# Cross-attention and quantized FFN on one core: the order of each engine's slots written anew

## The chip, the cores and the metric

One core of one Trainium2 chip. The time is the device time of one execution in microseconds (us); every table and row below is in us unless it says ns.

## The reference, cut to what matters

The input `x` is 64 x 64 rows of 256 (4096 rows, 32 tiles of 128 rows; a tile holds two sequences). All matrices are fp32.

```python
q_r    = layernorm(x) @ A            # Wq, w_kc_q, W_qr (and W_kr) are folded into one matrix per head, 16 heads
scores = q_r @ rope(kv).T            # per sequence and head, 64 x 64
attn   = softmax(scores)             # minus the row maximum, exp, divided by the row sum
ctx    = attn @ rope(kv)             # 64 columns per head
x      = x + ctx @ Bfold             # w_kc_kv and Wo folded: 1024 -> 256
h      = bitlinear(layernorm(x), w1) # rmsnorm, rows quantized to 8 bits, w1 to {-1,0,1}: 256 -> 1024
y      = x + bitlinear(gelu(h), w2)  # the same with w2: 1024 -> 256
```

## The kernel before, in words

All loops are unrolled in Python. Each engine has its own instruction stream, written out by hand as a loop over **slots** `n`, with semaphores between the streams. An engine works through its stream strictly in the order written: an instruction that waits holds back everything behind it on that engine. Slot `n` starts with the scores of tile `n`; older tiles are at later steps in the same slot. In a slot the stages are, with the tile that each works on before the change:

- **TensorE (PE)**: `scores(n)` (L707); two `queries` groups of 12 matmuls (L690 to L692) for coming tiles; `turned(n)` (L721), one transpose that turns the partial row maxima of tile n and the partial row sums of tile n-1 at once; `project(n-3)` (L754 to L756), 24 matmuls in two halves; `shifts(n)` (L734), which subtracts the row maxima from the scores in PSUM; `contexts(n-1)` (L744), which needs the division of tile n-2 to be through, since both use the two banks CB; `up(n-7)` (L776), 4 matmuls; `down(n-10)` (L786), 8 matmuls. Both ups of a pair lie around the border between an odd and an even slot.
- **VectorE (DVE)**: `quadrant_max(n)` (L923, two instructions), then `x_max(n-4)`, in even slots `norms` (14 small dependent instructions, L996, L196 to L201, L999, L1001), then `row_max(n)` (L936, tile nmax), `row_sum(n-1)` (L942, L946, tile ri), `divide(n-2)` (L953, two instructions, tile cr), `residual(n-3)`, maxima and scales of the FFN, `quadrant_sum(n)` (L930), `finish(n-10)` (L1007).
- **SyncE (SP)** issues the DMAs in order: `shift_rows(n)` (L343, nmax to shift), `rinv_rows(n-1)` (L351, the reciprocal sums to DRAM), `rinv_spread(n-1)` (L360, back from DRAM to 128 partitions, tile rb, waits for L351 to have landed), the transposes `turn_x` (L365) and `turn_g` (L370), the stores (L374). In slots 1 to 6 a 512 KB load of x (`load_x`) is issued between L343 and L351, and in slots 3 to 5 two `swap_kv` too.
- **ScalarE (ACT)**: `exp(n)`, `ctx_hi(n-2)` (L550), the copies of queries, `gelu(n-7)` (L565), squares. Exp and Gelu each need a table load when they follow the other.
- **GpSimd (POOL)**: `ctx_lo(n-2)` (L440), `centre(n-3)`, `x_round`, `g_round` (L463, L466), `norm_x` (L315), the rotation of kv (`rope`, L240 to L244) and rounding of w2 in the first slots.

Tile n's division thus needs `row_sum(n)` in slot n+1, the two DMA steps L351 and L360 in slot n+1, and stands in slot n+2:

```python
def divide(u, b):
    if b == 0:
        dve.wait_ge(sem["contexts"], u + 1)
        dve.wait_ge(sem["rinv_spread"], 32 * (u + 1))
```

Down uses columns 256 to 511 of the bank O, whose other half holds the projection. Four rounded FFN rows (g) and two of each transposed tile are kept. The loop runs over NT + 10 = 42 slots.

## Time and profile before

| what | us |
|---|---|
| median of 3 runs (455.26 to 457.75) | 455.36 |
| the profiled execution, device time | 457.08 |
| its span, first to last instruction | 454.9 |
| PE busy | 393.1 (86%) |
| DVE, ACT, POOL busy | 330.5, 257.8, 255.2 |
| mean granted PE clock | 0.957 |

Busy time is what the profiler records per instruction; matmuls overlap. A releaser behind "<-" is the instruction or DMA that ended an engine's idle time. R(n) stands below for the start of `row_max(n)`, the one L936 instruction of slot n; 32 of them mark the slots from R(0) = 39.2 to R(31). The span then has three parts: up to R(9) the start, with loads and few FFN steps; R(9) to R(31) the steady part; and the tail.

### The profile page before, as it was taken

To read this page: it belongs to the slowest core of one execution; us is meant where nothing else is said; L and a number is where in the kernel's file an instruction comes from. 1 tells how busy PE (TensorE), PEld (TensorE's weight loads), DVE (VectorE), ACT (ScalarE), POOL (GpSimd) and SP (SyncE) were. 2 spreads that over 40 slices of the span, in tenths; PEclk is the share of its full clock that TensorE was granted. 3 is DMA by queue.
4 is the path that set the end of the run, shared out by engine and by line. 5 is a ranking of instruction groups with operands and counts; after the bars stand their busy time and mean duration, and the time that the engine had idled before them with its cause. 6 is when DMAs were issued, how large, how long until landed. Compare 5 with 4: busy or idle time off the path is not lost.

```text
span 454.9 us, 8971 instructions
## 1 busy us (share of the span) xinstructions
PE 393.1 (86%) x2855; PEld 282.0 (62%) x2870; DVE 330.5 (73%) x873; ACT 257.8 (57%) x477; POOL 255.2 (56%) x321
## 2 busy tenths in 40 slices
PE   9799889794988999989999999999999997876554
PEld 7587557572665776767676767676767674464222
DVE  0364867584798789887878787878787888877564
ACT  1155543332667676675758585858585857556340
POOL 1209447994365656667373738373837373767543
PEclk9899999996999999999999999999999999999665
DMA  8993254443213232424262434252424253443333
GB/s 216 404 333 128 56 142 117 119 117 92 64 52 78 62 79 71 102 48 106 73 107 71 108 73 105 72 107 71 108 72 107 72 107 77 102 127 81 78 97 92
DMA packets 65533, 48.81 MB, mean 107 GB/s; under 512 B 50384, under 2 KB 55888, under 8 KB 65104
## 3 DMA queue, kind: packets, MB, share of 16 engines
q1 hardware_dynamic: 64880, 44.72, 37.8%
q10 hardware_dynamic: 608, 3.54, 2.3%
q8 instruction: 23, 0.38, 0.4%
q14 instruction: 22, 0.18, 0.2%
HBM read 31.98 MB, written 4.46 MB: 80 GB/s over the span
## 4 chain that ended last, share of the span: by engine, by line
POOL 34%; issue 31%; PE 15%; DMA 7%; DVE 6%; SPq 4%; ACT 1%; POOLq 1%; ACTq 0%; DVEq 0%
POOL cl L440 7%; POOL tq L463 6%; POOL qb L466 6%; POOL xa L455 3%; DMA wq_s<-wq 3%; POOL xq L458 3%; POOL yc L450 2%; POOL xn L315 2%; PE hps L786 2%; POOL w_s L478 2%; SPq L365 2%; DMA shift<-nmax 2%; PE ps L744 2%; PE ps L690 2%; DVE cr L953 1%
## 5 line engine op out<-in xcount | busy, mean ns | idle before, releaser
L440 POOL TENSOR_TENSOR cl<-cr,ch 128x512 fp32r<-128x512 f32 x64 | 80.3, 1277 | 131.0 <-ACT ch L550 131.0
L690 PE MATMUL ps<-xh,ah 128*128 128x256 f32 x256 | 75.6, 295 | 4.9 <-ACT g L565 4.5
L754 PE MATMUL hps<-bh,ch 128*128 128x256 f32 x256 | 76.7, 300 | 1.4 <-POOL cl L440 1.4
L534 ACT ACTIVATE qf<-ps 128x512 f32<-128x512 f32 x64 | 37.5, 586 | 65.4 <-PE ps L692 65.4
L755 PE MATMUL hps<-bl,ch 128*128 128x256 f32 x256 | 72.2, 282 | 0.0
L756 PE MATMUL hps<-bh,cl 128*128 128x256 f32 x256 | 72.2, 282 | 0.0
L691 PE MATMUL ps<-xl,ah 128*128 128x256 f32 x256 | 71.9, 281 | 0.0
L692 PE MATMUL ps<-xh,al 128*128 128x256 f32 x256 | 71.8, 280 | 0.0
L550 ACT ACTIVATE ch<-cr 128x512 fp32r<-128x512 f32 x64 | 39.3, 631 | 55.0 <-DVE cr L953 55.0
L690 PEld LDWEIGHTS ps<-xh,ah 128*128 128x128 f32 x256 | 48.2, 188 | 26.7 <-issue 25.8
L786 PE MATMUL hps<-w2q,qt 128*128 128x256 bf16 x256 | 39.1, 303 | 17.3 <-DMA qt<-qb 12.8
L786 PEld LDWEIGHTS hps<-w2q,qt 128*128 128x128 bf16 x256 | 25.0, 107 | 44.7 <-issue 24.4
L930 DVE TRANSPOSE_TENSOR_REDUCE red<-pe 128x16 f32<-128x512 f32 x64 | 41.6, 689 | 14.9 <-ACT pe L545 14.7
L565 ACT ACTIVATE g<-ps,scl 128x512 f32<-128x512 f32 x64 | 41.0, 683 | 19.6 <-PE ps L776 19.4
L923 DVE TRANSPOSE_TENSOR_REDUCE red<-hps 128x16 f32<-128x512 f32 x64 | 41.4, 685 | 12.6 <-PE hps L707 12.3
L754 PEld LDWEIGHTS hps<-bh,ch 128*128 128x128 f32 x256 | 48.4, 189 | 3.2 <-POOL cl L440 1.8
L755 PEld LDWEIGHTS hps<-bl,ch 128*128 128x128 f32 x256 | 48.4, 189 | 0.1
L756 PEld LDWEIGHTS hps<-bh,cl 128*128 128x128 f32 x256 | 48.3, 189 | 0.0
L692 PEld LDWEIGHTS ps<-xh,al 128*128 128x128 f32 x256 | 48.3, 188 | 0.0
L691 PEld LDWEIGHTS ps<-xl,ah 128*128 128x128 f32 x256 | 48.2, 188 | 0.0
L953 DVE TENSOR_TENSOR cr<-ps,rb 128x512 f32<-128x512 f32 x64 | 41.2, 686 | 7.2 <-DMA rb<-rinv_d 4.0
L776 PE MATMUL ps<-w1q,xqt 128*128 128x512 bf16 x113 | 35.1, 403 | 9.5 <-DVE xs L958 5.1
(136 smaller groups left out, 830.2 us busy)
## 6 DMA issues: line engine op xcount, KB each, us to landing
rb<-rinv_d SPq DMA_DIRECT2D x64, 256.0 KB, 3.9
xs<-x SPq DMA_DIRECT2D x8, 512.0 KB, 4.3
out<-yo SPq DMA_DIRECT2D x32, 128.0 KB, 3.5
wq_s<-wq SPq DMA_DIRECT2D x2, 1024.0 KB, 14.4
w_s<-w_t SPq DMA_DIRECT2D x2, 1024.0 KB, 7.2
wo_s<-wo_t ACTq DMA_DIRECT2D x1, 2048.0 KB, 11.1
wk_a<-wk_t SPq DMA_DIRECT2D x2, 512.0 KB, 7.3
kvs<-kvn SPq DMA_DIRECT2D x8, 128.0 KB, 4.1
```

Of the source, the lines that this page charges most:

```text
L440: pool.tensor_tensor(cl[:, u % 2, :, b * S:(b + 1) * S], cr[:, :, b * S:(b + 1) * S], ch[:, u % 2, :, b * S:(b + 1) * S].bitcast(F32), ALU ...
L565: act.activation(g[:, t % GB, 512 * half:512 * half + 512], turn_bank("h", t, half), ACT.Gelu, scale=hscale(scl, t)).then_inc(sem["gelu_do ...
L690: pe.matmul(o, ah[:, c, cols], xh[:, k % 2, c, :], start=(c == 0), stop=False)
L691: pe.matmul(o, ah[:, c, cols], xl[:, k % 2, c, :], start=False, stop=False)
L692: m = pe.matmul(o, al[:, c, cols], xh[:, k % 2, c, :], start=False, stop=(c == KC - 1))
L754: pe.matmul(O[:, 0:D], c_h, bh[:, hp, :], start=(hp == 0), stop=False)
L755: pe.matmul(O[:, 0:D], c_h, bl[:, hp, :], start=False, stop=False)
L756: m = pe.matmul(O[:, 0:D], c_l, bh[:, hp, :], start=False, stop=(hp == HP - 1))
L786: m = pe.matmul(O[:, D:2 * D], qt[:, t % 2, c, :], w2q[:, c, :], start=(c == 0), stop=(c == FC - 1))
L923: dve.tensor_reduce(red[:, u % 2, 16 * b:16 * b + 16], SB[b].rearrange("p (k s) -> p k s", s=32), AX.X, ALU.max, apply_transpose=True).the ...
L930: dve.tensor_reduce(red[:, (u + 1) % 2, 64 + 16 * b:80 + 16 * b], pe32[:, u % 2, b, :].rearrange("p (k s) -> p k s", s=32), AX.X, ALU.add, ...
L953: dve.tensor_tensor(cr[:, :, b * S:(b + 1) * S], CB[b].rearrange("p (h s) -> p h s", s=S), rb[:, b, :].rearrange("p (h s) -> p h s", s=S), ...
```

## The change

Every stream's slot is written in another order, and the distance of a tile behind its scores shrinks (NT + 6 = 38 slots):

- DVE: `divide(n-2)` is first in the slot, ahead of `quadrant_max(n)`; in odd slots the two `finish` of tiles n-6 and n-7 stand ahead of it. `residual(n-2)` is last (it was n-3, in the middle). In even slots `x_max(n-3)` and `x_scale` stand between `quadrant_max(n)` and `row_max(n)`.
- PE: `contexts(n-1)` moves from the end of the slot to after the scores and one queries group (even) or the two ups of tile n-5 (odd), ahead of `turned(n)`. Ups of tiles n-5 and n-4 both in odd slots, downs of n-5 and n-6 both in even slots; `project(n-2)`, one half or both behind the shifts. Downs of odd tiles go to the bank T. `x_t`, `fold_out` and `b_hi`, `b_lo` move by a slot.
- ACT: the four gelus of a pair in the odd slot with `ctx_hi` between; a dummy Gelu at the end of even slots loads the table.
- POOL: the rms norms move here from DVE, with `pow` in place of the Newton steps (six instructions); `x_round(n-4)`, `x_round(n-3)` in even slots, both `g_round` in odd ones. `norm_x(4)`, `norm_x(5)` run ahead of the loop.
- SP: `turn_g(n-5)` ahead of `shift_rows` in even slots, at the end in odd ones; `turn_x` behind `rinv_spread`; two stores ahead of `shift_rows` in odd slots. The issues `shift_rows(n)`, `load_x`, `swap_kv`, `rinv_rows(n-1)`, `rinv_spread(n-1)` keep their order.

```diff
@@ sync
-                for n in range(LAST + 1):
-                    if n % 2 == 0 and tile(n - 6):
-                        turn_x(n - 6)
-                        turn_x(n - 5)
-                    if n % 2 and tile(n - 10):
-                        turn_g(n - 10)
+                for n in range(LAST):
+                    if n % 2 == 0 and tile(n - 5):
+                        turn_g(n - 5)
+                    if n % 2 and tile(n - 7):
+                        store(n - 6)
+                        store(n - 7)
                     if tile(n):
                         shift_rows(n)
...
                     if tile(n - 1):
                         rinv_rows(n - 1)
                         rinv_spread(n - 1)
-                    if tile(n - 11):
-                        store(n - 11)
+                    if n % 2 == 0 and tile(n - 4):
+                        turn_x(n - 4)
+                        turn_x(n - 3)
+                    if n % 2 and tile(n - 5):
+                        turn_g(n - 5)
@@ tensor
                     if tile(n):
                         scores(n)
...
+                    if n % 2 and tile(n - 5):
+                        up(n - 5, 0)
+                        up(n - 5, 1)
+                    if n % 2 == 0 and k < NB:
                         queries(k, b)
+                    if tile(n - 1):
...
+                        contexts(n - 1)
+                    if n % 2 and tile(n - 5):
+                        up(n - 4, 0)
                     if n <= NT:
                         turned(n)
...
+                    if n % 2 == 0 and tile(n - 6):
+                        down(n - 5)
+                        down(n - 6)
@@ vector
                 for n in range(LAST):
...
+                    if n % 2 and tile(n - 7):
+                        finish(n - 6)
+                        finish(n - 7)
+                    if tile(n - 2):
+                        divide(n - 2, 0)
+                        divide(n - 2, 1)
                     if tile(n):
                         quadrant_max(n, 0)
                         quadrant_max(n, 1)
-                    if tile(n - 4):
-                        x_max(n - 4)
-                    if n % 2 == 0 and 0 <= (n - 6) // 2 < NB + 2:
-                        norms((n - 6) // 2)
+                    if n % 2 == 0 and tile(n - 4):
+                        x_max(n - 3)
+                        x_scale((n - 4) // 2)
                     if tile(n):
                         row_max(n)
                     if tile(n - 1):
                         row_sum(n - 1)
-                    if tile(n - 2):
-                        divide(n - 2, 0)
-                        divide(n - 2, 1)
...
+                    if tile(n - 2):
+                        residual(n - 2)
```

## Rows read from the trace of the kernel before

**Rows 1.** A stretch of two slots: busy time by engine, granted clock (--windows).

```profile
core 0: us, PE busy (x) PEld busy (x) DVE busy (x) ACT busy (x) POOL busy (x), PEclk, DMA share, GB/s
240.00:263.00 23.00, 21.86 (x173) 16.21 (x166) 18.12 (x47) 15.87 (x30) 13.09 (x16) 1.00 0.37 88
```

**Rows 2.** Timeline of VectorE, slots 18 to 20: start, length, what [idle before <-releaser].

```profile
245.12 0.28 DVE L936 TENSOR_REDUCE nmax<-hps 32x64 fp32r<-32x128 f32 x1 [0.32 <-PE hps L721]
...
255.79 0.28 DVE L936 TENSOR_REDUCE nmax<-hps 32x64 fp32r<-32x128 f32 x1 [1.42 <-PE hps L721]
...
257.00 1.29 DVE L953 TENSOR_TENSOR cr<-ps,rb 128x512 f32<-128x512 f32 x2
...
268.18 0.28 DVE L936 TENSOR_REDUCE nmax<-hps 32x64 fp32r<-32x128 f32 x1 [0.32 <-PE hps L721]
```

**Rows 3.** Timeline of SyncE's issues in slot 18.

```profile
246.92 0.81 SPq L351 DMA_DIRECT2D rinv_d<-ri  x2
248.75 1.31 SPq L360 DMA_DIRECT2D rb<-rinv_d  x2
```

**Rows 4.** DMA issues of the whole run: KB each, median us from issue to landing.

```profile
rb<-rinv_d SPq DMA_DIRECT2D x64, 256.0 KB, 3.9
...
xqt<-xq SPq DMA_TRANSPOSE x32, 2.9
qt<-qb SPq DMA_TRANSPOSE x32, 2.8
```

**Rows 5.** Timeline of VectorE in the start: slots 1, 2, 3, 4 and 9.

```profile
49.37 0.28 DVE L936 TENSOR_REDUCE nmax<-hps 32x64 fp32r<-32x128 f32 x1 [0.42 <-PE hps L721]
...
56.84 0.28 DVE L936 TENSOR_REDUCE nmax<-hps 32x64 fp32r<-32x128 f32 x1 [0.42 <-PE hps L721]
...
60.35 1.29 DVE L953 TENSOR_TENSOR cr<-ps,rb 128x512 f32<-128x512 f32 x2 [2.33 <-DMA rb<-rinv_d]
...
68.63 0.28 DVE L936 TENSOR_REDUCE nmax<-hps 32x64 fp32r<-32x128 f32 x1 [1.09 <-PE hps L721]
...
80.56 1.29 DVE L953 TENSOR_TENSOR cr<-ps,rb 128x512 f32<-128x512 f32 x2 [1.67 <-DMA rb<-rinv_d]
...
139.16 0.28 DVE L936 TENSOR_REDUCE nmax<-hps 32x64 fp32r<-32x128 f32 x1 [1.31 <-PE hps L721]
```

**Rows 6.** Timeline of SyncE's issues in slot 2, after its nmax.

```profile
62.53 1.31 SPq L360 DMA_DIRECT2D rb<-rinv_d  x2
```

**Rows 7.** Timeline of TensorE: contexts after a division, shifts of slot 6, an up.

```profile
61.79 0.61 PE L744 MATMUL ps<-pe,kvn 64*64 64x512 f32 x1 [0.42 <-DVE cr L953]
...
108.27 1.22 PE L734 MATMUL hps<-shift,em 128*128 128x512 f32 x2 [6.37 <-DMA shift<-nmax]
...
261.93 0.59 PE L776 MATMUL ps<-w1q,xqt 128*128 128x512 bf16 x2
```

**Rows 8.** Chain that ended last, in order of time: start, length, what.

```profile
110.34 1.91 PE ps L744 x8
...
133.40 1.02 PE ps L744 x8
...
450.37 1.88 PE hps L786 x8
```

**Rows 9.** Two us of slot 6, columns as in rows 1.

```profile
109.00:111.00 2.00, 2.00 (x10) 1.04 (x12) 1.27 (x3) 1.68 (x3) 0.11 (x1) 0.50 0.52 203
```

**Rows 10.** Timeline of GpSimd in slot 0: a rotation starts; later the norms.

```profile
40.27 1.28 POOL L240 TENSOR_TENSOR kvn<-kv_s,turn 128x512 f32<-128x512 f32 x1
...
44.25 2.07 POOL L315 TENSOR_SCALAR xn<-xs,rstd,nmean 128x256 f32<-128x256 f32 x2
```

**Rows 11.** Timeline of VectorE: the last nmax, of slot 31.

```profile
391.35 0.28 DVE L936 TENSOR_REDUCE nmax<-hps 32x64 fp32r<-32x128 f32 x1
```

**Rows 12.** Groups by line and form: xcount, busy, mean ns of one, idle before.

```profile
L440 POOL TENSOR_TENSOR cl<-cr,ch 128x512 fp32r<-128x512 f32 x64 | 80.3, 1277 | 131.0 <-ACT ch L550 131.0
...
L975 DVE TENSOR_REDUCE amax<-g 128x1 f32<-128x1024 f32 x32 | 37.4, 1212 | 0.0
...
L463 POOL TENSOR_SCALAR tq<-g,c 128x1024 f32<-128x1024 f32 x32 | 35.8, 1119 | 13.3 <-DVE c L982 10.9 <-POOL qb L466 2.4
```

More of the change, by code:

```diff
@@ L53, with norm_count @@
 YR = 4
-LAST = NT + 10
-NORM_STEPS = RSQRT_OPS + 3
+LAST = NT + 6
+def norm_count(j):
+    return sum(6 if 1 <= i < NB else 4 for i in range(j + 1))
 def build(nc, x, kv, wq, wk_t, wqr, wkr_t, wkv, wo_t, w1_t, w2_t, consts, out):
@@ L259, in build @@
             k, b = n // 2 + 1, 2 * (n % 2)
-            if n % 2 == 0 and tile(n - 7):
-                USES += [("h", n - 7, 0), ("h", n - 7, 1)]
+            if n % 2:
+                USES += [("h", t, half) for t in (n - 5, n - 4) if tile(t) for half in range(2)]
             if k < NB:
                 USES.append(("q", k, b))
-            if n % 2 and k + 1 < NB:
-                USES.append(("x", k + 1))
+            if n % 2 == 0 and n // 2 + 2 < NB:
+                USES.append(("x", n // 2 + 2))
             if k < NB:
@@ L269, in build @@
                 USES.append(("k", (n + 2) // 4))
-            if n % 2 and tile(n - 7):
-                USES += [("h", n - 7, 0), ("h", n - 7, 1)]
         def hscale(a, t):
@@ L424, in _ @@
                         swap_kv(n - 2)
-                    if n % 2 and tile(n - 9):
-                        turn_g(n - 9)
                     if tile(n - 1):
@@ L502, in _ @@
                 rope(pool, 1, sem["rope_steps"]).then_inc(sem["rope_done"], 1)
+                norm_x(pool, 4)
+                norm_x(pool, 5)
                 for n in range(LAST):
@@ L657, in _ @@
                         exp(n, 1)
+                    if n % 2 and k < NB:
+                        q_out(k, b + 1)
+                    if n % 2 and tile(n - 5):
+                        square_g(n - 5)
                     if turns(n):
@@ L904, in _ @@
                         fold_out(1)
-                    if turns(n):
-                        kv_t((n + 2) // 4)
-                    if tile(n - 1):
-                        if n == 1:
-                            pe.wait_ge(sem["b_lo_done"], 2)
-                        contexts(n - 1)
-                    if tile(n - 10):
-                        down(n - 10)
-                    if n % 2 and tile(n - 7):
-                        up(n - 7, 1)
+                    if n == 1:
+                        fold_out(3)
             @block.vector
@@ L1102, in _ @@
                         ternary(n)
+                    if n == 1:
+                        b_lo(2)
+                    if n % 2 == 0 and n // 2 + 2 < NB:
+                        x_lo(dve, n // 2 + 2)
+                    if n % 2 and tile(n - 3):
+                        x_max(n - 3)
+                    if n % 2 and tile(n - 5):
+                        for t in (n - 5, n - 4):
+                            g_max(t)
+                            g_scale(t)
+                    if n % 2 == 0 and 2 <= n < 14:
+                        statistics(dve, 4 + 2 * n, 8 + 2 * n)
                     if tile(n):
@@ L1105, in _ @@
                         quadrant_sum(n, 1)
-                    if tile(n - 10) and (n % 2 or not tile(n - 8)):
-                        finish(n - 10)
                     if n == 0:
                         b_lo(0)
-                    if n < 3:
-                        b_lo(n + 1)
-                    if 2 <= n < 14:
-                        statistics(dve, 4 + 2 * n, 6 + 2 * n)
+                        b_lo(1)
+                    if n == 1:
+                        b_lo(3)
+                    if tile(n - 2):
+                        residual(n - 2)
 def _constants():
```

244 lines of the change are left out of this document (119 added, 125 removed).

## The prediction

> **What bounds the kernel now.** I read the busy table first, then the windows, then the timeline of each engine in the same two slots, and last the DMA issues. In the steady part two slots take 268.18 - 245.12 = 23.06 us, and TensorE is busy for 21.86 of 23.00 us at full clock, DVE for 18.12, POOL for 13.09 [rows 1, 2]. So TensorE bounds it, with about 1.1 us of idle in two slots. That is all that any new order can win there: 11 pairs of slots lie between R(9) and R(31), so at most 11 x 1.2 = 13 us.
>
> The softmax chain runs beside it, and what matters is how much slack it has. From row_max(n) the chain to the division of tile n-1 is: reciprocal sums issued to DRAM 1.80 us after R(n) (246.92 - 245.12), the spread issued 1.83 later (the issue has waited for the first landing), its second DMA half a pair of issues later (0.65), and 3.9 to 4.2 until it has landed [rows 2 to 4]. I take 4.0, so the division of n-1 can start at R(n) + 8.3. Before the change the division comes later than that: in slot 18 the rows of tile 17 have landed at R(18) + 8.3 = 253.4, and its division starts in slot 19 at 257.00, behind R(19) = 255.79 [rows 2]. The slack is 3.6 us, and it exists because the division stands behind quadrant_max and row_max of its slot.
>
> In the start there is no such slack. DVE itself waits for rb in slot 2 (60.35, idle 2.33) and in slot 4 (80.56, idle 1.67). There R(1) = 49.37 leads to 60.35, a delay of 10.98, and R(3) = 68.63 to 80.56, a delay of 11.93 [rows 5]. For slot 2 the spread is issued at 62.53, 5.69 after R(2) = 56.84, which with 0.65 + 4.0 gives 10.4 [rows 5, 6]. The 2 to 3.6 us above 8.3 are the loads of x and the swaps of kv issued between L343 and L351.
>
> **The part that decides: the division first.** After the change row_max(n+1) stands behind divide(n-1), in order on DVE, and row_max(n) has to run before that division's data are on their way. So a loop closes: R(n) -> spread landed -> divide(n-1) -> quadrant_max(n+1) -> turned -> R(n+1). What each turn costs behind the landing:
> - Into an odd slot without ups: two divisions and two quadrant_max, 1.2 each pair to the next start and 1.3 to the last end, then transpose and start of nmax 0.35: 2.85. The two divisions' 1.29 stand in [rows 5]; quadrant_max I take equally long, since both read 128 x 512.
> - Into an odd slot with ups (n of 5 and more) TensorE is later than DVE: contexts wait for the division and start 0.15 after its end (61.79 against 60.35 + 1.29) [rows 5, 7], take 1.02 [rows 8], one up half takes 0.53 (261.93 to the scores of 262.46; the row's 0.59 is its length) [rows 7], then transpose and nmax 0.31: 3.3.
> - Into an even slot x_max and x_scale (0.7 together, an estimate from the small instructions) stand ahead of row_max: 3.15.
>
> **Steady part.** A pair of slots needs 2 x 8.3 + 3.3 + 3.15 = 23.05 us by the loop, against 23.06 now and 21.9 by TensorE. The gain that the denser TensorE order could bring is eaten by the loop. Over 22 slots 22 x 11.53 = 253.6 against 391.35 - 139.16 = 252.2 now [rows 5, 11]: **+1.4**.
>
> **Start.** norm_x(4) and (5) run ahead of the loop, 4 us earlier than before, but x_t(2) moves to slot 0, where TensorE gets to it about 39.2. The norms can start only at 40.3 and take 1.1 to 2.1 us [rows 10]; TensorE stands about 2.4 us, and with b_lo(1) ahead of contexts(0) and quadrant_max(1) the slot 1 slips: R(1) = 52.8 in place of 49.37, **+3.4**. Then the loop: delays to the division from R(1) to R(8) are 10.98, 10.4, 11.93, then 12.0 in slots 4 and 5 (loads and swaps as in slot 3), 10.4 in slot 6 (load only), 8.3 and 8.3: sum 84.3. The rest into R(2) to R(9) is 2 x 2.85 + 3 x 3.3 + 3 x 3.15 = 25.1. So R(9) = 52.8 + 109.4 = 162.2, against 139.16 now [rows 5]: **+23** with the 3.4.
>
> TensorE now idles 4 to 6 us in each of slots 2 to 6, waiting for the division before contexts. In slot 6 of the trace the granted clock is 0.50, the 1.2 GHz level, behind an idle of 6.37, and eight context matmuls take 1.91 in place of 1.02 [rows 7 to 9]. These lie in the loop, so I add 0.8 x 5 = **+4**. The Trainium skill (TensorE: Matmul & The Clock Gate, HAM oscillation) says the same of loops that wait for a DMA in each turn: the engine falls back to half clock every time. By that rule the whole 4 us are due, by the row of slot 6 alone only when the idle is as long as there; without it the start is +23.
>
> **Tail.** From R(31) = 0: division(30) at 8.3, contexts(31) end cold at 11.8, row_sum(31) 13.1, rb(31) lands at 13.1 + 1.85 + 0.65 + 4.0 = 19.6. Gelus of pair 28, 29 and ctx_hi stand between, ctx_lo (1.28) ends at 25.0. POOL then rounds g of 28 and 29 (4 x 1.1), 29.5; centre(31), x_max, x_scale, x_round to 33.0; transposed by 36.3 (two issues, 2.9). Up and gelu of 31 end at 38.9, its maximum and scale at 40.5, rounded 43.3, transposed 46.4 (2.8), two cold downs of 1.9, finish 0.5, store 2.1: 53.0 [rows 4, 8, 12]. Now it is 454.9 - 391.35 = 63.55 [rows 11]: **-10.5**. The shorter pipeline wins here: three to four tiles' FFN steps fewer are left.
>
> **Moves without a price.** The norms leave DVE: 14 small instructions in an even slot, which now end before nmax (it waits 0.32 for the transpose behind them [rows 2]), so nothing is won while that wait stays. On POOL six instructions, 2.3 us as an estimate with one pow of 1.0, lie in 10 idle us of a pair [rows 1]; if the cover goes, gelu of the next odd slot is late by at most that. The gelus in the middle of the odd slot push exp to R + 5.4, ahead of the next scores at R + 6.4; without that cover about 0.5 a pair. Downs in pairs, bank T, stores first in odd slots, turn_g ahead of shift_rows: rounded g is ready some 3 us before that issue; bounds 0 to +0.5 us a pair, I take 0. The number of table loads stays.
>
> **Sum.** 23 + 4 + 1.4 - 10.5 = +17.9, so the span goes from 454.9 to 472.8 and the profiled execution from 457.08 to 475.0. That execution lies 1.7 above the median of the three runs, so against 455.36 I predict **473 us**.
>
> **Rivals.**
> - A, the loop in the start only: rb lands quicker and the steady part falls to TensorE's 21.9. Then 473 - 12.7 - (cold clock) 4 = 456, or 460 if the cold stays. For it: rb takes 3.9 in the median with other traffic about. Against: the 4.2 of many spreads.
> - B, faster: no loop, the divisions find their rows landed as they do now in the steady part. Place: R to division in slots 1 to 8. Point of decision: a turn must average 11.4 us instead of 14.2, so the landing must be some 2.8 us earlier there. Then the start keeps its present 89.8 us less the stall of slot 6 (6.4 [rows 7], where the shifts wait behind other work of SyncE and DVE), and the tail's 10.5 come in whole: 455.4 + 3.4 + 1.4 - 10.5 - 6.4 = 443. Against: two waits for rb already stand in that stretch [rows 5].
> - C, worse: SyncE's order adds to the loop. If turn_g ahead of shift_rows, or transposes in front of it, cost 0.6 a slot over 22 slots, it is 473 + 13 = 486.
>
> **Chances.** Forecast 0.65, A 0.11, B 0.14, C 0.10. The range of 456 to 484 takes in the unknown bounds (cold clock 0 or 4, landing 3.9 or 4.2 over 30 turns = 9 us, steady part down to TensorE's bound) and leaves out B. About 1% is what a measurement tells from no change: slower by over 1% 0.79, within it 0.07 (the lower end of A and the upper of B), faster 0.14.
>
> **What would show it.** In the trace after: DVE cr waits for DMA rb in nearly every slot, some 1 to 5 us in slots 2 to 7; nmax follows nmax by 13 to 15 us in slots 1 to 6 and by 11.5 after slot 8; PE's contexts (L744 before) wait for cr; R(1) near 53, R(9) near 163 to 167, last nmax to the end near 53. Wrong if R(9) stays below 150, or if DVE doesn't wait for rb, or if pairs fall below 22.5 us.

## The result, and the profile after

| | before | after |
|---|---|---|
| median of 4 runs (lowest to highest) | 455.95 (455.26 to 457.75) | 504.77 (501.81 to 508.05) |
| the profiled execution, device time | 457.08 | 508.05 |
| its span | 454.9 | 506.2 |
| mean granted PE clock | 0.957 | 0.919 |

The ratio is 1.107, 95% interval 1.098 to 1.115: slower by 49 us. The direction is the predicted one. The size is not: 473 was forecast, with 484 as the upper end. The profiled execution, from which all rows below come, is the longest of its four and lies 3.3 above their median. One execution further below, of the kernel with single columns (499.96 us), was in the slow state and is left out of that kernel's median.

The start of row_max of slots 1, 9 and 31 splits both spans into the three parts that the prediction used. Timeline of VectorE after the change (start, length, what, idle before and its releaser), first the slots 1 and 2, then slots 9, 15 to 17 and 31. Here and in the fences below, rows in between are left out:

```profile
54.88 0.28 DVE L971 TENSOR_REDUCE nmax<-hps 32x64 fp32r<-32x128 f32 x1 [0.42 <-PE hps L745]
65.85 1.29 DVE L988 TENSOR_TENSOR cr<-ps,rb 128x512 f32<-128x512 f32 x2 [4.91 <-DMA rb<-rinv_d]
69.71 0.28 DVE L971 TENSOR_REDUCE nmax<-hps 32x64 fp32r<-32x128 f32 x1 [1.35 <-PE hps L745]
...
173.67 0.28 DVE L971 TENSOR_REDUCE nmax<-hps 32x64 fp32r<-32x128 f32 x1 [0.70 <-PE hps L745]
...
258.14 1.29 DVE L988 TENSOR_TENSOR cr<-ps,rb 128x512 f32<-128x512 f32 x2 [1.09 <-issue]
259.35 1.30 DVE L958 TRANSPOSE_TENSOR_REDUCE red<-hps 128x16 f32<-128x512 f32 x2
260.57 0.38 DVE L998 TENSOR_REDUCE amax<-yc 128x1 f32<-128x256 f32 x1
260.98 1.14 DVE L1004 SCALAR_TENSOR_TENSOR gm<-amax,level 128x2 f32<-128x2 f32 x1
262.24 0.28 DVE L971 TENSOR_REDUCE nmax<-hps 32x64 fp32r<-32x128 f32 x1
270.79 1.29 DVE L988 TENSOR_TENSOR cr<-ps,rb 128x512 f32<-128x512 f32 x2 [1.21 <-DMA rb<-rinv_d]
274.00 0.28 DVE L971 TENSOR_REDUCE nmax<-hps 32x64 fp32r<-32x128 f32 x1 [0.70 <-PE hps L745]
...
451.40 0.28 DVE L971 TENSOR_REDUCE nmax<-hps 32x64 fp32r<-32x128 f32 x1 [0.70 <-PE hps L745]
```

| part | before | predicted | after |
|---|---|---|---|
| R(1) | 49.37 | 52.8 | 54.88 |
| R(9) | 139.16 | 162.2 (+4 for the clock) | 173.67 |
| R(9) to R(31) | 252.2 | 253.6 | 277.7 |
| R(31) to the end | 63.55 | 53.0 | 54.8 |

So 34.5 us of the difference in the spans (51.3) arose in the start and 25.5 in the steady part, and the tail gave 8.7 back. Against [rows 2]: there the division comes 1.21 after the row_max of its own slot, with no idle before it; here it stands first in the slot and DVE idles before it. The list of waits of the whole run says it for all slots (us in total, times, longest):

```profile
DVE cr L988 <- issue: 35.3, 17, 6.6
...
PE ps L768 <- DVE cr L988: 30.7, 26, 4.9
...
PE ps L800 <- DMA xqt<-xq: 23.6, 13, 6.9
```

On the page the same wait has a second releaser, and "issue" only says that the profile shows none: the tile's own view gives `DMA rb<-rinv_d` 22.6 us in 13 times beside the 35.3 in 17, 30 waits in 32 divisions. In the start the chain that ended last shows the loop itself, here from slot 1 to 7, and with two rows from slot 11 (start, length, what):

```profile
57.41 2.97 DMA rinv_d<-ri
61.13 4.22 DMA rb<-rinv_d
67.28 1.98 PE ps L768 x8
72.36 3.15 DMA rinv_d<-ri
76.22 1.56 DMA rb<-rinv_d
77.80 2.80 issue
82.03 1.98 PE ps L768 x8
108.97 4.11 DMA xqt<-xq
113.52 1.49 PE ps L800 x3
115.01 1.92 PE ps L768 x8
...
146.98 1.79 PE ps L768 x8
...
191.18 4.97 DMA xqt<-xq
198.03 1.86 PE ps L768 x8
```

Store the reciprocals, spread them, contexts behind the division, and again: one turn a slot. In slots 5, 7 and 11 the last link is not the spread but the transposed x (`xqt`), which is issued behind the spread and which the ups ahead of contexts wait for. From slot 13 on the chain view runs along GpSimd, with gaps of up to 6.5 us that it calls "issue", and shows the loop no longer; for the steady part the waits above, the sum below and the experiments have to carry it. TensorE goes cold in the loop. Two windows of 2 us with contexts of slots 2 and 5, and one with the contexts of a warm slot (columns as in [rows 9]):

```profile
67.20:69.20 2.00, 1.92 (x9) 0.34 (x9) 1.16 (x2) 1.08 (x3) 1.91 (x2) 0.50 0.01 4
114.90:116.90 2.00, 2.00 (x10) 0.35 (x10) 0.46 (x1) 1.21 (x2) 0.57 (x1) 0.50 0.00 0
284.90:286.10 1.20, 1.05 (x8) 0.24 (x8) 1.20 (x3) 1.20 (x4) 1.05 (x1) 1.00 0.41 75
```

The clock is 0.50, the 1.2 GHz level, in both cold windows, and eight context matmuls take 1.98 and 1.92 in the chain where the warm ones take 1.05.

Two slots of the steady part, to be held against [rows 1], take 25.46 in place of 23.06 us, with the same work on TensorE. TensorE no longer bounds them:

```profile
262.24:287.70 25.46, 21.62 (x163) 15.86 (x163) 17.80 (x37) 15.26 (x30) 15.42 (x22) 1.00 0.39 80
```

**One turn, measured.** For each slot I read R to the division, and the division to the next R. Means over R(9) to R(31), 22 slots:

| | predicted | measured | slots | us |
|---|---|---|---|---|
| R to division | 8.3 | 8.95 (even), 8.85 (odd) | 22 | +13.2 |
| division to R of an odd slot | 3.3 | 3.47 | 11 | +1.9 |
| division to R of an even slot | 3.15 | 3.99 | 11 | +9.2 |

The sum is +24.3, and the miss in the steady part is 277.7 - 253.6 = 24.1. These terms cover the whole slot, so the sum has to come out; what it shows is where the miss sits. The +1.9 comes from the turns into two slots, 11 and 25, which took 4.66 and 4.60 where most take 3.21: there the ups waited 2.2 and 2.3 us for the transposed x, and the contexts behind them ran at a granted clock of 0.55 and 0.50. The experiments had to show that these terms are causes and not places where something else is waited out.

### The profile page after: what moved, and what is told of

The parts are those of the page before. It is cut to its first block, busy times and chain, and to the rows that moved or that the text cites. A ratio compares the mean times of both kernels' runs of the same rounds, so it can differ in the third digit from the quotient of the medians.

```text
span 506.2 us, 8902 instructions
## 1 busy us (share of the span) xinstructions
PE 407.0 (80%) x2854; PEld 294.7 (58%) x2870; DVE 302.9 (60%) x653; ACT 261.6 (52%) x499; POOL 292.2 (58%) x417
## 3 DMA queue, kind: packets, MB, share of 16 engines
q1 hardware_dynamic: 64880, 44.72, 36.7%
## 4 chain that ended last, share of the span: by engine, by line
issue 30%; POOL 30%; DMA 15%; PE 8%; SPq 8%; DVE 6%; POOLq 1%; ACT 1%; DVEq 0%
POOL cl L427 8%; POOL tq L450 6%; DMA rinv_d<-ri 5%; DMA rb<-rinv_d 4%; POOL qb L453 3%; SPq L329 3%; DMA wq_s<-wq 3%; DMA xqt<-xq 3%; PE ps L768 2%; POOL fw L474 2%; POOL xa L442 2%; POOL yc L437 2%; DVE cr L988 2%; SPq L346 2%; POOL xn L301 2%
## 5 line engine op out<-in xcount | busy, mean ns | idle before, releaser
L713 PE MATMUL ps<-xh,ah 128*128 128x256 f32 x256 | 78.0, 305 | 3.4 <-ACT g L579 3.1
L988 DVE TENSOR_TENSOR cr<-ps,rb 128x512 f32<-128x512 f32 x64 | 41.2, 686 | 57.9 <-issue 35.3
L780 PE MATMUL hps<-bh,cl 128*128 128x256 f32 x256 | 74.8, 292 | 0.0
L779 PE MATMUL hps<-bl,ch 128*128 128x256 f32 x256 | 74.8, 292 | 0.0
L768 PE MATMUL ps<-pe,kvn 64*64 64x512 f32 x128 | 41.6, 723 | 31.3 <-DVE cr L988 30.7
L713 PEld LDWEIGHTS ps<-xh,ah 128*128 128x128 f32 x256 | 50.5, 197 | 22.6 <-issue 12.6
L778 PEld LDWEIGHTS hps<-bh,ch 128*128 128x128 f32 x256 | 51.7, 202 | 8.9 <-POOL cl L427 7.6
L800 PE MATMUL ps<-w1q,xqt 128*128 128x512 bf16 x112 | 35.5, 419 | 24.6 <-DMA xqt<-xq 23.6
L779 PEld LDWEIGHTS hps<-bl,ch 128*128 128x128 f32 x256 | 51.8, 202 | 1.4
L559 ACT ACTIVATE pe<-hps 128x512 f32<-128x512 f32 x64 | 34.7, 594 | 34.6 <-PE hps L758 34.6
L780 PEld LDWEIGHTS hps<-bh,cl 128*128 128x128 f32 x256 | 51.6, 202 | 0.0
L814 PE MATMUL hps<-w2q,qt 128*128 128x256 bf16 x256 | 34.3, 291 | 12.1 <-DMA qt<-qb 12.1
```

The source lines that it names most:

```text
L713: pe.matmul(o, ah[:, c, cols], xh[:, k % 2, c, :], start=(c == 0), stop=False)
L768: m = pe.matmul(CB[b][dst, :], (kvn, kvs)[gg][src, u, :], pe32[src, u % 2, b, :], start=True, stop=True, skip_group_check=True)
L778: pe.matmul(O[:, 0:D], c_h, bh[:, hp, :], start=(hp == 0), stop=False)
L779: pe.matmul(O[:, 0:D], c_h, bl[:, hp, :], start=False, stop=False)
L780: m = pe.matmul(O[:, 0:D], c_l, bh[:, hp, :], start=False, stop=(hp == HP - 1))
L988: dve.tensor_tensor(cr[:, :, b * S:(b + 1) * S], CB[b].rearrange("p (h s) -> p h s", s=S), rb[:, b, :].rearrange("p (h s) -> p h s", s=S), ...
```

## The experiments

Medians of each kernel and of the kernel before on the same chip; "ratio" is to the kernel before, with its 95% interval. Theory L: the new order closes the loop R(n), spread landed, division(n-1), R(n+1), and the time is the length of its turns. Rival T: the new order of TensorE and the shorter distances cost the time, and the divisions' waits are only a symptom. Each of the first four kernels below was run twice, all others four times.

**One part alone: the division first, in the kernel before.**

```diff
@@ vector, kernel before
+                    if tile(n - 2):
+                        divide(n - 2, 0)
+                        divide(n - 2, 1)
                     if tile(n):
                         quadrant_max(n, 0)
                         quadrant_max(n, 1)
...
-                    if tile(n - 2):
-                        divide(n - 2, 0)
-                        divide(n - 2, 1)
```

> The kernel before with one edit: on VectorE divide(n-2) stands ahead of quadrant_max(n). Theory L (the loop row_max -> DMA round trip -> division -> next row_max sets the slot): row_max to the next division 8.5 to 8.9 us in the steady part, then 2.9 to the next row_max into odd slots and about 5.9 into even ones (the norms stand there in this kernel): a pair 26 us, 22 slots 286 in place of 252, the start 119 in place of 90: about 515 us. Rival T (the shorter distances and the new order of TensorE cost the time, the divisions' waits are only a symptom): this kernel keeps TensorE's order and the distances, so it stays within 2%, at most 465 us.

573.55 us, ratio 1.257 (1.251 to 1.263). This one edit costs 117 us, more than the whole change, and T's 465 at most is far off. Timeline of VectorE, three slots of it:

```profile
305.46 0.28 DVE L936 TENSOR_REDUCE nmax<-hps 32x64 fp32r<-32x128 f32 x1
315.22 1.29 DVE L953 TENSOR_TENSOR cr<-ps,rb 128x512 f32<-128x512 f32 x2 [0.40 <-issue]
318.15 0.28 DVE L936 TENSOR_REDUCE nmax<-hps 32x64 fp32r<-32x128 f32 x1
328.23 1.29 DVE L953 TENSOR_TENSOR cr<-ps,rb 128x512 f32<-128x512 f32 x2 [3.83 <-DMA rb<-rinv_d]
335.68 0.28 DVE L936 TENSOR_REDUCE nmax<-hps 32x64 fp32r<-32x128 f32 x1
```

The mechanism is L's, the size is not. R to division takes 10.2 in the mean of the 22 slots, 10.5 in the odd ones, where turn_g stands between L343 and L351, and 9.8 in the even ones; 8.5 to 8.9 was expected. Division to R takes 7.3 in the mean into even slots (7.45 here), since the norms, which in the kernel before cost nothing, now stand in the loop; 5.9 was expected.

**The round trip taken out.** The spread is read from a constant in DRAM and issued ahead of shift_rows, so the contexts are not divided by their row sums.

```diff
@@ sync, changed kernel
-                    at_least(sp, sem["rinv_spread"], 32 * (u - 1))
...
-                    sp.wait_ge(sem[f"rinv_stored{p}"], 32 * (u // 2 + 1))
...
-                        rows = rinv_d[p, :, :, :].rearrange("b g n -> (b g) n")[half:4 - half:3 - 2 * half, :]
+                        rows = consts[0:4, 0:512][half:4 - half:3 - 2 * half, :]
...
+                    if tile(n - 1):
+                        rinv_spread(n - 1)
                     if tile(n):
                         shift_rows(n)
...
                         rinv_rows(n - 1)
-                        rinv_spread(n - 1)
```

> The changed kernel, but rb is spread from an input constant and issued ahead of shift_rows, so no division waits for row sums (the softmax isn't divided by its sums; those and their issue to DRAM stay). Theory L: the slots fall to what TensorE needs, some 11 us, the start to about 88 us between R(1) and R(9), the tail loses about 4: 445 us within 10. Rival T: the ups still wait for their transposed tiles and the order of TensorE is the same, so it stays above 490 us.

469.80 us, ratio 1.030 (1.023 to 1.036). Some 35 of the 49 us go; both theories miss their bounds, L's 455 by 15 and T's 490 by 20. The steady part takes 260.4 and R(1) to R(9) 102.4 us, both above the kernel before. One late pair takes 23.67 us, but the pair from slot 9 to 11 takes 26.77, at a granted clock of 0.94.

In the even slots from 6 to 26 the issues of turn_g and of the spread (1.38 us), which both stand ahead of shift_rows, end behind the row_max: after R(10) = 167.07 the shift is issued at 168.00, 0.93 later, and 0.31 is the usual distance. So this kernel holds its own shifts back, and 35 us may be less than the loop costs.

**Single terms of the loop.** First x_max and x_scale, in even slots, behind row_sum:

```diff
@@ vector, changed kernel
-                    if n % 2 == 0 and tile(n - 4):
-                        x_max(n - 3)
-                        x_scale((n - 4) // 2)
                     if tile(n):
                         row_max(n)
                     if tile(n - 1):
                         row_sum(n - 1)
+                    if n % 2 == 0 and tile(n - 4):
+                        x_max(n - 3)
+                        x_scale((n - 4) // 2)
```

> The changed kernel with x_max and x_scale behind row_sum in even slots. Theory L: division to row_max in even slots falls from 4.1 to about 2.9 us, 1.2 x 14 even slots: 16 us less, 488. The 1.1 us of the first x_scale instruction no longer lie in the loop, wherever it stands. Rival T: row_max a little earlier wins nothing: 502 to 506 us.

493.08 us, ratio 1.081 (1.073 to 1.088): 11.7 less. Division to R into even slots is 2.93 in place of 3.99, and L1004 takes 0.16 in most of them. Then the loads:

```diff
@@ sync, changed kernel
-                    if 1 <= n < 7:
-                        load_x(n + 1)
-                    if n in (3, 4, 5):
-                        sp.wait_ge(sem["rope_done"], n - 2)
-                        swap_kv(n - 2)
                     if tile(n - 1):
                         rinv_rows(n - 1)
                         rinv_spread(n - 1)
+                    if 1 <= n < 7:
+                        load_x(n + 1)
+                    if n in (3, 4, 5):
+                        sp.wait_ge(sem["rope_done"], n - 2)
+                        swap_kv(n - 2)
```

> The changed kernel with load_x and swap_kv behind rinv_spread on SyncE. Theory L: row_max to division in slots 1 to 6 falls from 10.9 to 12.6 us to about 9, together some 15 us less, R(9) near 159, 489 us. Rival T: the same loads, so at most 3 us less.

496.35 us, ratio 1.088 (1.074 to 1.101): 8.4 less, though with two runs, 493.8 and 498.9, the interval touches that of the changed kernel. In the profile R(1) to R(9) takes 108.6 in place of 118.8. Both together:

> The changed kernel with both single edits together: x_max and x_scale behind row_sum in even slots (alone -11.7), load_x and swap_kv behind rinv_spread (alone -8.4). They sit at different places of the loop (one between division and row_max in every even slot, the other between row_max and the landing in slots 1 to 6), so theory L says they add: 485 (482 to 489). If something else than the loop set the slots, the second would bring less than half of its own: 489 to 493.

482.78 us, ratio 1.060 (1.054 to 1.066). The edits add: 504.8 - 11.7 - 8.4 = 484.7, and the loads bring 10.3 here, clear of the noise. In slot 6 the next stall comes up: shift_rows stands 3.85 us behind its row_max, held by the transposes of g ahead of it (116.40, 4.30 for two), which is the place of rival C.

**Why x_scale takes so long.** Its first instruction L1004 has a tile of 128x2 and takes 1.11 us in the median of 16. GpSimd's timeline over the same stretch of the changed kernel:

```profile
259.58 2.53 POOL L427 TENSOR_TENSOR cl<-cr,ch 128x512 fp32r<-128x512 f32 x2 [0.67 <-ACT ch L564]
...
278.11 1.13 POOL L450 TENSOR_SCALAR tq<-g,c 128x1024 f32<-128x1024 f32 x1
```

L1004 of that slot starts at 260.98 and ends at 262.12, and ctx_lo ends at 262.11. g_scale's first instruction, 128x1 with two operands, runs from 278.41 for 0.83 and ends at 279.24, exactly with the L450 of this fence. So they seem to wait for a GpSimd instruction in progress. The Trainium skill (SBUF — State Buffer, Who interferes with whom) says that GpSimd and VectorE share one pair of ports as an exclusive lock, which a VectorE instruction with two SBUF inputs wants against a GpSimd one that reads SBUF. The first test took the second input away:

```diff
@@ vector, changed kernel, x_scale
-dve.scalar_tensor_tensor(out=gm[:, c], in0=amax[:, p, 0:2], scalar=FLOOR1, in1=level[:, 0:2], op0=ALU.max, op1=ALU.mult).then_inc(sem["x_scale_steps"], 1)
+dve.tensor_scalar(gm[:, c], amax[:, p, 0:2], FLOOR1, -1.0 / 127.0, ALU.max, ALU.mult).then_inc(sem["x_scale_steps"], 1)
```

> The changed kernel, with the first instruction of x_scale (128x2, 1.11 us in the median of 16, standing between division and row_max in even slots) written with the constant -1/127 as an immediate in place of the tile level: the same place, the same value, one operand from SBUF in place of two. Theory P (the instruction waits for GpSimd's ctx_lo because both want the port that the engines share, and only an instruction of two SBUF operands has to): it takes 0.2 us in place of 1.11, and over 14 even slots in the closed loop 14 x 0.9 = 12.6 us go: 492 (490 to 497). Theory W (it is slow because it waits for x_max's result or for its place in the order, whatever its operands): it still takes 1.1 us and the time is within 2 us of the changed kernel, 503 to 507.

504.49 us, ratio 1.106 (1.098 to 1.115): nothing, and the instruction still ends with ctx_lo (259.13, 2.52 here). The row of VectorE:

```profile
260.54 1.14 DVE L1004 TENSOR_SCALAR gm<-amax 128x2 f32<-128x2 f32 x1
```

Theory P as I had put it fell. W's time came true, but W had no reason for an end at the same 0.03 us as GpSimd's. The same page says that a tensor_scalar can run in a mode with two ports and then contends too. The condition stands in the Trainium skill (VectorE: DVE Perf Modes, Mode 2×_2P): source and destination in SBUF and an even outermost dimension, so that each port reads one half. So the second test split the two columns:

```diff
@@ vector, changed kernel, x_scale
-dve.scalar_tensor_tensor(out=gm[:, c], in0=amax[:, p, 0:2], scalar=FLOOR1, in1=level[:, 0:2], op0=ALU.max, op1=ALU.mult).then_inc(sem["x_scale_steps"], 1)
...
+dve.tensor_scalar(gm[:, 2 * p:2 * p + 1], amax[:, p, 0:1], FLOOR1, -1.0 / 127.0, ALU.max, ALU.mult).then_inc(sem["x_scale_steps"], 1)
+dve.tensor_scalar(gm[:, 2 * p + 1:2 * p + 2], amax[:, p, 1:2], FLOOR1, -1.0 / 127.0, ALU.max, ALU.mult).then_inc(sem["x_scale_steps"], 1)
```

> The changed kernel, x_scale in its place between division and row_max, its first instruction (128x2) split into two tensor_scalar of 128x1 each with the constant as an immediate. With one operand at 128x2 it still took 1.11 us, so the number of operands is not what makes it wait. The Trainium skill (SBUF — State Buffer, the shared port pair) has a tensor_scalar wait for a GpSimd instruction only in a mode in which both read ports serve one tensor, which one element per partition cannot be split for. If that is the mechanism: 2 x 0.17 us in place of 1.11, 14 even slots x 0.8 = 11 us less, 493 (491 to 497). If any write or read of DVE waits for GpSimd there, or x_max's result is what is late: still 1.1 us or more, 503 to 508.

494.43 us (median of three), ratio 1.083 (1.073 to 1.093): 10.3 less than the 504.77 of the changed kernel. In the profile the steady part is 8.8 shorter, and division to R into even slots takes 3.24 in place of 3.99. VectorE's timeline, from x_scale to row_max:

```profile
253.10 0.15 DVE L1004 TENSOR_SCALAR gm<-amax 128x1 f32<-128x1 f32 x1
253.17 0.14 DVE L1005 TENSOR_SCALAR gm<-amax 128x1 f32<-128x1 f32 x1
253.35 0.17 DVE L1007 RECIPROCAL c<-gm 128x2 f32<-128x2 f32 x1
253.43 0.28 DVE L971 TENSOR_REDUCE nmax<-hps 32x64 fp32r<-32x128 f32 x1
```

GpSimd's in the same stretch:

```profile
251.69 2.53 POOL L427 TENSOR_TENSOR cl<-cr,ch 128x512 fp32r<-128x512 f32 x2 [0.84 <-ACT ch L564]
```

Both instructions run in the middle of ctx_lo, which lasts to 254.22, and so do the row_max and the reciprocal, which has two columns and one operand. So the form decides whether an instruction waits. Of the forms seen here the one with two operands and the tensor_scalar of two columns do; the tensor_scalar of one column, the reductions and the reciprocal do not.

> The same with load_x and swap_kv behind rinv_spread. If both terms are the loop's, this gives 8 us less than the run with single columns alone: 485 (481 to 489), as the pair of x_scale late and loads late gave 482.78. If the single columns change nothing: 496.

487.53 us, ratio 1.065 (1.057 to 1.073), inside the expectation: 6.9 less than single columns alone.

**The loop opened in the changed kernel.** On ScalarE ctx_hi(n-2) also moves, behind the four gelus, in even slots behind the first q_out.

```diff
@@ vector, changed kernel
-                    if tile(n - 2):
-                        divide(n - 2, 0)
-                        divide(n - 2, 1)
                     if tile(n):
                         quadrant_max(n, 0)
                         quadrant_max(n, 1)
-                    if n % 2 == 0 and tile(n - 4):
-                        x_max(n - 3)
-                        x_scale((n - 4) // 2)
...
                         row_sum(n - 1)
+                    if tile(n - 2):
+                        divide(n - 2, 0)
+                        divide(n - 2, 1)
+                    if n % 2 == 0 and tile(n - 4):
+                        x_max(n - 3)
+                        x_scale((n - 4) // 2)
@@ tensor
-                        contexts(n - 1)
...
-                    if n % 2 == 0 and tile(n - 2):
-                        project(n - 2, 0)
                     if tile(n):
                         shifts(n)
+                    if tile(n - 1):
...
+                        contexts(n - 1)
...
-                    if n % 2 and tile(n - 2):
+                    if tile(n - 2):
                         project(n - 2, 0)
-                    if tile(n - 2):
                         project(n - 2, 1)
```

> The changed kernel with the loop opened and nothing else undone: the division stands behind row_max and row_sum again, contexts (and with them both halves of the projection) behind shifts, ctx_hi behind the gelus or the first copy. Pairs of ups and gelus in odd slots, downs in even ones, norms on GpSimd, the new SyncE order and the short distance of six to seven slots stay. Theory L: R(9) near 140, a slot of the steady part 11.4 (251 over 22), the last row_max to the end about 57: 448 (440 to 458), all of the 49 us back. Rival T (other parts of the new order, the GpSimd norms and the shared port among them, hold the steady part): 475 or more, with 12 or more a slot.

514.92 us, ratio 1.130 (1.121 to 1.139). A clear miss of L's 448; of the two it is T's forecast (475 or more, 12 or more a slot) that came true. The division finds its rows again (1.21 after R, no wait), and yet a slot takes 13.3. Its two kinds of slots:

```profile
302.84:314.52 11.68, 10.74 (x83) 8.09 (x82) 9.30 (x18) 7.22 (x15) 8.05 (x9) 1.00 0.28 70
314.52:329.68 15.16, 12.90 (x82) 8.21 (x81) 8.57 (x18) 7.92 (x16) 7.34 (x14) 0.89 0.33 79
```

With the division behind row_max, ctx_lo comes late, and the projection of tile n-2 can only run behind the shifts. In the even slot shifts start 3.9 after R (1.73 of idle for their DMA), and contexts, projection and both downs all follow; the next scores start 8 us later. SyncE's timeline there:

```profile
312.02 3.67 SPq L356 DMA_TRANSPOSE qt<-qb  x2
315.77 1.40 SPq L329 DMA_DIRECT2D shift<-nmax  x2
```

The shift is issued 1.25 after R(20) = 314.52, not 0.31, since the transposes of g stand ahead of it: rival C's place. In slots 8, 10, 12 and 14 it comes 3 us after R, and TensorE waits for the shift 36.9 us in the run, 15 times, against 9.6 us in 9 in the changed kernel. So this kernel has a stall of its own, and how much of its time comes from the short distance, how much from where I put contexts and projection, and how much from turn_g, no run parts. What it shows is narrower: taking the loop out of this kernel in this way costs 10 us and gives nothing back.

> The kernel with the loop opened, and load_x and swap_kv behind rinv_spread as well. With the loop open a late landing in slots 1 to 6 has about 3 us of slack, so theory L gives less than the 8.4 us that this edit brought in the closed loop: 0 to 3 us below the run with the loop opened alone. If the loads cost by traffic and not by their place in the queue: no difference in either kernel beyond 1 us.

513.82 us, ratio 1.126 (1.118 to 1.134), 1.1 below the one before, within their spreads. The same edit brings 7 to 10 us in the closed loop and about nothing here, as L says of a landing with slack.

**SyncE's order in the kernel before.**

```diff
@@ sync, kernel before
-                    if n % 2 == 0 and tile(n - 6):
-                        turn_x(n - 6)
-                        turn_x(n - 5)
                     if n % 2 and tile(n - 10):
                         turn_g(n - 10)
...
                         rinv_spread(n - 1)
+                    if n % 2 == 0 and tile(n - 6):
+                        turn_x(n - 6)
+                        turn_x(n - 5)
```

> The kernel before with one edit of the change's SyncE order alone: the transposes of x stand behind rinv_spread in place of ahead of shift_rows. In the kernel before the shifts of slot 6 wait 6.37 us for the shift DMA, and there the issue stands behind turn_x. Theory L (the change loses its time in the loop through the division, the SyncE order itself costs nothing): 448 to 456, the stall of slot 6 gone. Rival T (the new SyncE order costs time by itself, 0.3 to 0.6 a slot): 462 or more.

450.11 us, ratio 0.988 (0.983 to 0.992), 5.8 below the kernel before on the same chip: there this part of the change is a gain. The wait of the shifts of slot 6 [rows 7] shrinks from 6.37 to 3.41. With the loads late too:

> The kernel before with SyncE's transposes of x and the loads of x and swaps of kv all behind rinv_spread (the first of these alone brought 5.4). In the kernel before the division has slack in the steady part but waits for the spread 2.33 us in slot 2 and 1.67 in slot 4, where the loads stand between the two issues. Theory L: those waits go, 2 to 5 us below the run with the transposes alone: 447 (445 to 449). If the open order has slack enough there: 450, no difference.

448.95 us, ratio 0.987 (0.981 to 0.993), the best of all kernels here. The 1.2 us between it and the one before are less than their spread and the ratios are the same, so the two expectations are not told apart. R(1) to R(9) went from 86.2 to 81.9, and of VectorE's two waits for rb there that of slot 4 is gone and 1.9 of the 2.33 in slot 2 is left, but the steady part went from 248.5 to 250.9.

**The landing moved.** The spread as one DMA in place of two; rinv_rows stores the rows of b = 1 in reversed order to fit.

```diff
@@ sync, rinv_spread
-                    for half in range(2):
-                        rows = rinv_d[p, :, :, :].rearrange("b g n -> (b g) n")[half:4 - half:3 - 2 * half, :]
-                        sp.dma_start(rb[64 * half:64 * half + 64, :, :], rows.partition_broadcast(64)).then_inc(sem["rinv_spread"], 16)
+                    rows = rinv_d[p, :, :, :].rearrange("h b n -> h (b n)").unsqueeze(1).to_broadcast([2, 64, 1024])
+                    sp.dma_start(rb[:, :, :], rows).then_inc(sem["rinv_spread"], 16)
...
```

> The changed kernel with rinv_spread written as one DMA of 256 KB in place of two of 128 (the rows lie in DRAM in the order that one source pattern can read). Its second issue ends 0.65 us after the first, and the division waits for the second. Theory L (R to division is in the loop one for one in every slot from 1 to 31): 0.65 a slot, 30 slots, 20 us less, 485 (480 to 491), and R to the division falls from 8.9 to about 8.2 in the mean. If instead something beside the loop ends last in the steady part: less than half of it, above 495, with the landing earlier and an idle before the next nmax that has another releaser. If one DMA of twice the size lands as late as the second of two: no change of either.

(By the profile the sizes are 512 KB and two of 256 KB; the expectation halves them.) 769.97 us, ratio 1.690 (1.680 to 1.701). My expectation of the DMA was wrong: what waits for it starts 12.65 after its issue (259.92 to 272.57), where the two took 5.1 in the mean. The issue in SyncE's timeline:

```profile
259.92 0.55 SPq L345 DMA_DIRECT2D rb<-rinv_d  x1
```

And VectorE's timeline around it:

```profile
252.29 1.29 DVE L987 TENSOR_TENSOR cr<-ps,rb 128x512 f32<-128x512 f32 x2 [9.00 <-issue]
256.36 0.28 DVE L970 TENSOR_REDUCE nmax<-hps 32x64 fp32r<-32x128 f32 x1
272.57 1.29 DVE L987 TENSOR_TENSOR cr<-ps,rb 128x512 f32<-128x512 f32 x2 [7.29 <-DMA rb<-rinv_d]
277.06 0.28 DVE L970 TENSOR_REDUCE nmax<-hps 32x64 fp32r<-32x128 f32 x1 [1.98 <-PE hps L744]
```

As a test of the loop it is a large dose in place of a small one, and not a pure one, since other transfers slow down beside it (below). R to the division takes 16.45 in the mean, 7.55 more than in the changed kernel, and a slot of the steady part 20.95 in place of 12.62, 8.33 more. So the changed kernel has no slack at this point: the delay is in the path in every slot, and some 0.8 of other delays with it. The same edit in the kernel before with the transposes and the loads late:

> The same edit in the kernel before, with the transposes of x and the loads late as in the run that gave 448.95. There the division has about 3.6 us of slack in the steady part, so theory L says an earlier landing is worth nothing there and at most 0.65 in each of the slots of the start: 447 (445 to 449.5). If the landing is on the path in the kernel before too: 440 or less.

600.52 us, ratio 1.318 (1.310 to 1.327). The steady part takes 347.3, a slot 15.8, which is 4.4 more than the 11.4 of the same kernel with two issues, against 8.3 more in the changed kernel. That the order before absorbs a part fits the slack of 3.6 that the prediction read from the trace [rows 2], but it is no measure of it: in odd slots the spread itself was issued only 9.6 to 11.9 after R here, against 5.2 to 6.3 with two issues.

> The changed kernel with three edits: single columns in x_scale, loads late, the spread in one issue. If all three are terms of one loop they add: 487.5 - 20 = 468 (462 to 475), near the run without the round trip (469.8); the loop then turns in about 11.5 us, and the TensorE order takes over. If they do not add: 478 or more.

760.13 us, ratio 1.665 (1.652 to 1.679). With the spread this late the run can't show the sum that it was made for. R(1) to R(9) is 10.2 shorter than with one issue alone, the loads' share. The steady part is only 1.4 shorter: division to R into even slots takes 3.86 in place of 4.07, so at the half clock the contexts end last there, and of the faster x_scale only 0.2 is left.

## Why the prediction was right in direction and wrong in size

- **The part that decides** was right. The loop exists and DVE waits in 30 of 32 divisions. The division moved alone costs 117 us; without the round trip 35 of the 49 us go; a delay of 7.55 in R to division comes out as 8.33 a slot.
- **The step that failed is the steady part, "+1.4".** It was the sum 2 x 8.3 + 3.3 + 3.15 = 23.05, set against 23.06 by the kernel before, and the real pair takes 25.25. Its mechanism held; two of its terms were mis-sized. Of the 33 us by which the profiled execution missed its 475.0, 24 lie here, 7.5 in the start and 1.8 in the tail.
  - "The division of n-1 can start at R(n) + 8.3": measured 8.9, worth 13.2 us over 22 slots. 8.3 lies below all that is seen, 8.39 to 9.77. The sum had 3.63 to the spread's issue and 4.65 from there. In 17 slots the second part took 4.93 in the mean, worth some 5 us; in the other five (10, 13, 17, 22, 23) 5.5 to 6.1, worth 6; and in slots 12, 19, 24, 25, 28 and 23 the spread was issued 0.15 to 0.75 late, worth 3. A median of landings (3.9 before, 4.0 after, from 3.6 to 5.3) is the wrong statistic for a loop, which pays the late ones and gets nothing back for early ones. The landing was named among the bounds ("landing 3.9 or 4.2 over 30 turns = 9 us") but put in at the lower side.
  - "x_max and x_scale (0.7 together, an estimate from the small instructions)": measured 1.7, of which 1.11 is one instruction of 128x2 that waits for ctx_lo. Worth 9.2 us. The moves behind row_sum (-11.7) and to single columns (-10.3) show it. The prediction gave no row for the 0.7, and the change puts x_scale straight behind the division, where ctx_lo always runs.
- **The start** was 7.5 us too low of 27. R(1) came at 54.88 and not 52.8 (+2.1), which is within what R(1) varies by itself: 51.1 to 55.3 over the profiles of the changed kernel and of its variants that differ from it only later. The eight delays to the division sum to 86.2 against 84.3 (+1.9). The rest into the next R is 32.6 against 25.1 + 4 with the clock (+3.5). Of this 5.20 is slot 4 to 5, where in the chain the ups wait for the transposed x (6.92 us of idle; L800 waits 23.6 us in all) ahead of contexts. That ups stand ahead of contexts in the loop had been priced, that they might wait for their own DMA had not.
- **The clock** was right in kind: half clock in the contexts of slots 2 to 7 (0.50 to 0.59), and into slots 2 and 3 the turn took 3.86 where 2.85 was put in without it. But into the even slots 4 and 6 it cost nothing: 4.07, as in the warm even slots of the steady part, since x_scale ended last. And the steady part, for which none was put in, had two cold slots, 11 and 25. The rule of the Trainium skill that the prediction names (TensorE: Matmul & The Clock Gate, HAM oscillation) is borne out here for the start. In three slots of the steady part (contexts at 259.57, 272.22, 285.05) the idle ahead of them was 0.27 to 1.41 us, and the two slots from 262.24 ran at 1.00; it is not so that every turn fell to half clock.
- **The tail** was right within 1.8 (54.8 against 53.0), and step by step too: the last division starts at 20.3 where rb(31) was put at 19.6, and the last rounding ends at 45.4 against 43.3.
- **The moves without a price.** In this kernel the terms of the loop leave nothing over for them in the steady part; with the round trip out, 13.2 us remain that may be theirs. Of SyncE's, the transposes of x behind rinv_spread are worth 5.8 us to the kernel before. Rival C's place (turn_g ahead of shift_rows) is real but hidden in this kernel, where the shift is issued 0.3 after R in every slot: it showed in slot 6 of the run with both edits, by up to 0.7 without the round trip, and by 0.8 to 5 in the even slots 6 to 26 with the loop opened. So the 486 of C would have been nearer in number, for a reason that did not act.
- Rivals A and B asked for an earlier landing than the sum had, and fell with the same rows.

**Still open.** What makes the five late landings late. In all five a fetch of instructions lies on the DMA queues between the spread's issue and the division, and in 16 of the other 17 slots none does (slot 11 has one and was on time). In the runs with late loads, with one operand and with single columns every slot of the steady part in which this stretch took over 5.45 us has such a fetch too, slots 17 and 23 each time, but others with a fetch were on time, and no run took the fetches away. Why the spread was issued late in six slots, no run shows. What of the 13.2 us that remain without the round trip comes from that kernel's own early issue, and what from the new order, no run parts. And why the kernel with the loop opened is slower than the changed one is argued, not shown: moving turn_g behind shift_rows in it was not tried.

## What to carry to other kernels

Before you move a consumer ahead of its producer's successor, draw the circle: if the moved step waits for a DMA that is started behind it, slack of some us turns into a term of every turn, and everything in between (a norm, a scale, a load's issue) is then paid in full. Price such a circle with the mean or the late side of the landings, not the median, and price small VectorE instructions in it with what GpSimd will be doing beside them in the new order. Ask of every step that stands in it whether it waits for a DMA of its own. A shorter pipeline wins once, in the tail (8.7 us here); a loop loses in every slot.

## What the runs showed of the hardware that was not expected

- A 128x2 instruction of VectorE took 1.11 us in place of 0.16 because a GpSimd tensor_tensor was in progress. It did so with two SBUF operands and with one; split into 128x1 pieces it took 0.15 and 0.14, while ctx_lo ran on GpSimd, and a 128x2 reciprocal took 0.17 there. A 128x1 instruction with two operands waited too (0.83). The Trainium skill has both rules (SBUF — State Buffer, Who interferes with whom), and the rows agree.
- One DMA of 512 KB with a source of two rows of 4 KB, each repeated 64 times, was landed some 12 us after its issue; two of 256 KB land in 4.0 in the median. A window in the middle of it (columns as in [rows 1]) shows how few of the core's 16 DMA engines worked:

```profile
266.00:268.00 2.00, 0.00 (x0) 0.00 (x0) 0.00 (x0) 0.00 (x0) 0.00 (x0) 1.00 0.13 51
```

  A DMA share of 0.13 is that of two engines of 16, and 51 GB/s over 10 us are 0.5 MB, the whole transfer. In the changed kernel the two DMAs move 200 to 250 GB/s at 267 to 269 us. What picked two, no run here shows; the outermost dimension of the source pattern is 2 as well.
- The transposes issued behind this DMA took 12.2 and 6.0 us in place of 3.6 and 3.1. The queue's line (packets, MB, share of 16 engines' span) went from 36.7% in the changed kernel to this, for the same bytes (44.72 and 44.71 MB):

```profile
q1 hardware_dynamic: 61872, 44.71, 56.5%
```

  Windows with a share above 1 (3.57 at 264 to 266 us) show that it also counts time in which a packet only waits, so it does not say that the engines worked longer.
